# Graph layers on one core: the semaphore of an aggregation step raised by a drain behind the matmuls

## What is computed

```
# GAT
a   = softmax over the edges of one target of leaky_relu(el[src] + er[dst])
rst = segment_sum(feat_v[src] * a, dst)            # aggregation 1
# GCN, twice
h   = x @ W
agg = segment_sum(h[src] * norm, dst)              # aggregations 2 and 3
x   = relu(agg + h * self_weight + b)
```

## Time and profile before

| | us |
|---|---|
| median of three runs | 5063.07 (5060.97 to 5071.13) |
| span of the profiled execution | 5032.2 |
| GAT aggregation (about 915 to 2254) | 1339 |
| GCN aggregation 1 (about 2471 to 3645) | 1174 |
| GCN aggregation 2 (about 3855 to 5022) | 1167 |
| busy over the span: PE / DVE / ACT / POOL | 3834.1 / 2339.5 / 2192.4 / 2436.2 |

### The profile page before, as it was taken

One profiled execution on the slowest core, in us unless ns is written; L12 is line 12 of the kernel. 1 busy time (PEld: TensorE's weight loads), 2 busy tenths in 40 slices (PEclk: granted clock), 3 DMA queues, 4 the chain that ended last, 5 costly groups with the idle time before them and its releaser, 6 DMA issues.

```text
span 5032.2 us, 77636 instructions
## 1 busy us (share of the span) xinstructions
PE 3834.1 (76%) x18550; PEld 2250.0 (45%) x18551; DVE 2339.5 (46%) x4398; ACT 2192.4 (44%) x5340; POOL 2436.2 (48%) x2548
## 2 busy tenths in 40 slices
PE   4679998667667667779777777777897777777777
PEld 3369983455555555554323333333343333333333
DVE  5358887556566566668422222222353222222226
ACT  3236542334344444445444444444543444444444
POOL 3510000555555555543466666666503666666666
PEclk8889999888888888889888888899998888888989
DMA  7522325555555555555566665666514666666668
GB/s 247 169 60 59 84 53 182 153 158 156 154 157 152 143 146 146 151 146 196 185 178 181 174 177 170 170 177 174 158 75 144 182 178 179 175 170 172 177 174 305
DMA packets 317266, 803.60 MB, mean 160 GB/s; under 512 B 67665, under 2 KB 97251, under 8 KB 316241
## 3 DMA queue, kind: packets, MB, share of 16 engines
q0 software_dynamic: 193760, 629.95, 43.7%
q1 hardware_dynamic: 94981, 120.30, 7.6%
q10 hardware_dynamic: 28428, 52.40, 3.1%
HBM read 718.21 MB, written 85.04 MB: 160 GB/s over the span
## 4 chain that ended last, share of the span: by engine, by line
PE 56%; another core or an unknown queue 17%; issue 12%; ACT 6%; DVE 3%; ACTq 2%; DMA 2%; DVEq 1%; SPq 1%; POOL 1%; POOLq 0%
PE mm L1661 12%; PE tr L1661 11%; PE mm L1491 7%; PE mm L1638 4%; PE sm L1638 4%; PE mm L1583 4%; PE tr L1583 4%; ACT eler_hots L1392 2%; PE sm L1528 2%; ACT eler_hots L1383 2%; PE tr L1638 2%; PE hist_ps L1638 2%; PE tr L1486 1%; DVE big L857 1%
## 5 line engine op out<-in xcount | busy, mean ns | idle before, releaser
L1250 POOL DMA_INDIRECT edge<-h_tab,src_group x1564 | 1491.3, 954 | 1079.9 <-issue 431.7
L1392 ACT ACTIVATE eler_hots<-eler_hots,ones 128x256 f32<-128x256 f32 x1320 | 663.8, 503 | 1177.8 <-remote 622.4
L1661 PE MATMUL mm<-edge,eler_hots 128*128 x1760 | 923.3, 669 | 308.5 <-ACT eler_hots L1392 152.5
L1661 PE MATMUL tr<-edge,eler_hots 128*128 x1760 | 916.5, 664 | 277.8 <-DVE big L857 109.4
L1250 POOL DMA_INDIRECT rows_wmat<-v_tab,src_group x782 | 739.0, 945 | 636.7 <-DVE edge L831 375.8
L1383 ACT ACTIVATE eler_hots<-iota,ndrel 128x128 f32<-128x128 f32 x2640 | 916.0, 393 | 173.8 <-issue 9.1
L1661 PEld LDWEIGHTS mm<-edge,eler_hots 128*128 128x128 f32 x1760 | 367.4, 214 | 835.9 <-issue 830.7
L1661 PEld LDWEIGHTS tr<-edge,eler_hots 128*128 128x128 f32 x1760 | 364.9, 212 | 799.7 <-issue 799.7
L857 DVE TENSOR_TENSOR big<-big,mm 128x512 f32 x440 | 302.8, 688 | 894.3 <-remote 347.1
L857 DVE TENSOR_TENSOR big<-big,tr 128x512 f32 x440 | 302.7, 688 | 827.8 <-remote 371.0
L1638 PE MATMUL mm<-edge,eler_hots 128*128 128x260 f32 x1176 | 423.3, 446 | 308.7 <-ACT eler_hots L1392 206.5
(11 more groups left out here) (234 smaller groups left out, 3873.8 us busy)
## 6 DMA issues: line engine op xcount, KB each, us to landing
h_tab<-rows_wmat SPq DMA_DIRECT2D x98, 256.0 KB, 2.0
edge<-h_tab,src_group POOLq DMA_INDIRECT x1564
rows_wmat<-low_tab SPq DMA_DIRECT2D x191, 128.0 KB
ht_tab<-rows_wmat SPq DMA_DIRECT2D x49, 256.0 KB
big<-ht_tab ACTq DMA_DIRECT2D x49, 256.0 KB
v_tab<-rows_wmat ACTq DMA_DIRECT2D x49, 256.0 KB
x_tab<-big SPq DMA_DIRECT2D x49, 256.0 KB, 2.1
rows_wmat<-v_tab,src_group POOLq DMA_INDIRECT x782
```

The source lines that it names most:

```text
L1250: pool.indirect_dma_start(ring[:, 2 * u + c, :], None, tab, bass.IndirectOffsetOnAxis(ap=src_group[:, n:n + 1], axis=0)).then_inc(a["rows_ ...
L1392: act.activation(onehot[:, s.j % 2, :, :], dist[:, :, :], ACT.Relu, bias=ones[:, 0:1], scale=-1.0).then_inc(a["onehot_set"], 1)
L1661: last = pe.matmul(sum_ps[bank][:, :], onehot[:, s.j % 2, n, :], edge[:, ds(slot[0][s.j] + n * D, D)], start=(n == 0), stop=(n == 1))
```

## The change

In all three aggregations the last matmul of a step no longer raises `step_sum`. Behind the step's matmuls PE gets a drain, and the drain raises it. That is 440 drains in each of the three aggregations, 1320 in all. The waits for `step_sum` and their values stay. No other instruction changes its place on any engine; the drain stands between the last matmul of one step and the waits and the first weight load of the next.

```diff
--- before.py
+++ after.py
@@ -1635,9 +1635,9 @@
                         pe.wait_ge(a["acc_added"], 2 * (w - PAIRS + 1))
                     for n in range(2):
                         for bank_ps, lo, hi in ((sum_ps[bank], 0, AW // 2), (half_ps[bank], AW // 2, AW)):
-                            last = pe.matmul(bank_ps[:, 0:hi - lo], onehot[:, s.j % 2, n, :], msgs[:, s.j % MSGS, n, lo:hi],
+                            pe.matmul(bank_ps[:, 0:hi - lo], onehot[:, s.j % 2, n, :], msgs[:, s.j % MSGS, n, lo:hi],
                                              start=(n == 0), stop=(n == 1))
-                    last.then_inc(a["step_sum"], 1)
+                    pe.drain().then_inc(a["step_sum"], 1)
                 pipelined(pe, SP, 4 * PAIRS, 0, step)
 
             def aggregate(a):
@@ -1658,9 +1658,9 @@
                     if s.past(BANKS):
                         pe.wait_ge(a["acc_added"], w - BANKS + 1)
                     for n in range(2):
-                        last = pe.matmul(sum_ps[bank][:, :], onehot[:, s.j % 2, n, :], edge[:, ds(slot[0][s.j] + n * D, D)],
+                        pe.matmul(sum_ps[bank][:, :], onehot[:, s.j % 2, n, :], edge[:, ds(slot[0][s.j] + n * D, D)],
                                          start=(n == 0), stop=(n == 1))
-                    last.then_inc(a["step_sum"], 1)
+                    pe.drain().then_inc(a["step_sum"], 1)
                 pipelined(pe, SP, OFFS, 0, step)
 
             all_placed(pe)
```

## The result

The changed kernel took 5498.17 us (median of four, 5490.55 to 5507.03); the kernel before took 5062.02 us beside it. The ratio is 1.087, with a 95% interval of 1.0845 to 1.0894. So the change costs 436 us, where the prediction had 217 us, and lies 8 us above the end of its range. The direction was right, the size was half.

The account below looks back on a forecast made before the run. The prediction took the aggregations to be bound by POOL's gathers plus pauses after late `step_sum` raises. With a 0.5 us gap, pauses of 747.5 us grow by 0.29, 217 us: 5063 + 217 = 5280 us; overall range 4650 to 5490 us.

Parts of the forecast that it names:

- What bounds the kernel now: Aggregations: POOL's 977.5 us each plus pauses, 747.5 us together; PE's quick GCN step 1.72 us, POOL's 2.22.
- I take it that the drain is as late as the matmul was: Raise of `step_sum` in the aggregations: the drain's raise comes no earlier than the matmul's, so late stretches stay.
- The rival in which the drain's raise goes another way: Aggregations: the drain's raise avoids the lateness, so 380 us less, 4683 us; chance 0.34.
- The gap: PE between two steps, behind each of 1320 drains: 0.5 us taken, 0.41 least, about 1.0 most.
- my four rows: PE's gap: tail 0.16 us, knowing the end 0.10, first weight load 0.25, waits and drain 0.16; together 0.67.
- The sum: Aggregations: 1.29 times as many periods with equal pauses, 217 us more: 105 in GAT, 57 and 55 in GCN.
- my rule: Aggregations: pauses grow as PE's step lengthens; 217 us at a 0.5 us gap, 432 us at 1.0.
- The clock held: PE's granted clock in the aggregations: should hold; well below 0.85 would break the sum.
- Nothing else paid: Aggregations: one-hot making (0.69 + 0.51 us) and DVE's add (0.69) stay under a 2.22 us step, costing nothing.
- the signs that I had named: Aggregations: "remote" waits stay or grow, quick-stretch gap 0.4 to 1.0 us, POOL's ring waits 240 us or more per GCN layer.
- the faster case: Aggregations: "remote" waits vanish because the drain is not late; 380 us less, 4683 us; chance 0.34.
- The last rival: Aggregations: every step pays 0.5 us and no late stretch shortens, 660 us more, 5720 us; chance 0.06.

Follow-up runs that it names:

- the single-gather run: Kernel before, with only the first gather of each unit issued in GCN 2: 759 us there from first to last record.
- the run with small pauses: Kernel before, with a small POOL memset behind every second gather in GCN 1 and every gather in GCN 2: ratio 1.0027.
- the single-gather run with drains: Changed kernel, with only the first gather of each unit issued in GCN 2: 1198 us there, no late raise.

## Why the prediction had the direction and missed the size

**What bounds the kernel now**: PE's quick step of 1.72 us is shown by the single-gather run, which keeps it for a whole layer. It is not what a layer with two gathers could run at: POOL's 2.22 us a step, an estimate, lies above it. With one gather a unit the late raises go from 53 to 2. POOL's time plus pauses, on which the sum was built, did not hold as a rule: in the run with small pauses POOL's time grew and the layer did not.

**"I take it that the drain is as late as the matmul was"**: the drain's raise comes 0.02 us later in a quick step, and is late less often. With drains the GCN layers had half the late raises, and just as few with the matmul's raise and an idle drain, or with a wait. The rival in which the drain's raise goes another way had no part in it.

The Trainium skill, "PSUM — Partial Sum Buffer", section "Engine vs sequencer instructions", says that a drain waits for the engine to go fully idle. The traces agree: each step stands alone behind a drain, and a wait for the step's own semaphore gives nearly the same picture, at 1.072 against 1.087.

**The gap is the step that failed.** "I take 0.5 us: tail, knowledge and load, with the waits counted as mostly met beforehand." Measured, it is 1.0 us, the most that I had named. Its parts in the timeline after: 2.38 - 1.72 = 0.66 us in every step; 0.12 us more in three steps of eight, where the wait for rows stands, 0.05 a step; and 4.16 - 2.38 = 1.78 us more at the head of each turn of eight, 0.22 a step. That is 0.93 of the 1.0 us; in the single-gather run the clock of 0.97 goes with the rest.

The 0.66 us equal the sum of my four rows (0.67), but not row by row: the tail is 0.16 us as I had it, the end is known after 0.15 us, not 0.10 (3008.09 to 3008.24), the waits take 0.25 us, not 0.16, and the weight load 0.10 us, not 0.25. That the four sum so well is luck. The waits were the term that I left out of the value taken: each takes 0.04 us, and 0.05 to 0.06 us lie between two, which I had not counted. A wait that was met long ago still has to be gone through, and so has a table load; both were free only while a matmul was running. The table loads I left without a price because no row showed them.

**The sum** then took a wrong road. It let the late stretches come 1.29 times as often and grow by 105 us in GAT and by 57 and 55 us in the GCN layers. They shrank instead: in GCN 1 from 57 events to 27, in GAT from 398 us of DVE's idle time to 272. What cost the time is that PE became the bound, with 1197.6 / 440 = 2.72 us a step in the single-gather run with drains, beyond POOL's 2.22. A GCN layer now has 439 us of gaps, of which 170 us show in GCN 1 and 149 us in the run with drains in GCN alone.

Where the other 269 us went can be counted in two ways, and the runs do not decide between them. Along PE's queue, the late raises of GCN 1 fell by 359 - 85 = 274 us. Against POOL's pace, an estimate from the earlier trace rows of 977.5 us a layer, PE had 977.5 - 759 = 218 us of room before it became the slower one, and the time beyond the slower one fell from 1173 - 977.5 = 196 us to 1343 - 1198 = 145 us.

With a gap of 1.0 us my rule would have given 432 us, near the 436 measured, but by 207 us in GAT and 114 and 110 in the GCN layers, where 126, 170 and 173 us are right. It would have been right by accident.

**The other points.** The clock held (0.92 in the GCN layers against 0.88), as forecast. Nothing else paid: in the GCN layers ACT and DVE have the same busy time. Of the signs that I had named, POOL's waits for the ring (361.8 us) and the gap came out as for the forecast; the waits for a late raise did not stay or grow. Of the faster case the fewer late raises came true, but not by its mechanism, and the gap cost more than they gave. The last rival put the gaps on the path in full at 0.5 us: PE does pay them in every step, at 1.0, but less than half of it shows in a layer.

**What stays open** is what makes a raise late. It all but stops with one gather a unit (2 events for 53), and it isn't a matter of the gathers' bytes (half the rows, no change) or of a break of 0.09 us between them. With drains it gets rarer. Whether the number of TensorE instructions matters is not clear: with twice as many, 86 events for 54 by my mark, but only 79 waits of DVE on "remote" for 68. With one gather a unit POOL also waits at the ring between gathers, so the number of gathers and the pauses between them were not told apart. A wait taken from the gathers themselves was not tried.

## What to carry to other kernels

A raise by the last matmul lets the next step's waits, register loads and weight load run under this step's columns; a drain or a wait that makes TensorE wait for its own end uncovered all of them at once here (1.087 and 1.072). Price such a gap by everything that stands in that queue between the two steps, met waits and loop heads included, each at its own duration and with the 0.05 to 0.06 us to the next, not by the pipeline's tail. And if a kernel has a second loss that depends on pace, measure the first with the second taken away: here 439 us of gap stood behind 170 us that showed.

## What the runs showed that I had not expected

- A gather of 64 rows takes POOL 711.67 / 774 = 0.92 us on average in its layer (the first 16 there have 128 rows), one of 128 rows 734.42 / 775 = 0.95 us: almost all of it is by instruction.
- A drain and a wait on the engine's own semaphore cost nearly the same, 0.06 us apart.
- With one gather a unit, and hardly a late raise, a GCN layer runs in 759 us where it takes 1170 us with two. That is not what the late raises cost: 782 gathers at POOL's pace take 977.5 us by themselves, an estimate from the earlier trace rows. So ending the late raises alone would win some 196 us of GCN 1's 1173 at most, unless the gathers went faster as well.
